# Self-attention's last two units: low parts, two 16-bit copies a unit and the weight splits laid out again on VectorE

## What is computed

```python
q = proj(w_q); k = proj(w_k); v = proj(w_v)
qn = _rmsnorm(q, q_gamma) * dh ** (-0.5)
kn = _rmsnorm(k, k_gamma)
sim = jnp.einsum('bhid,bhjd->bhij', qn, kn)
attn = jax.nn.softmax(sim, axis=-1)
out = jnp.einsum('bhij,bhjd->bhid', attn, v)
```

## Time before and its profile

| | us |
|---|---|
| median of 3 runs | 2266.23 (2263.83 to 2267.96) |
| the profiled execution | 2270.32 |
| its span | 2268.5 |
| PE busy | 2161.2 |
| ACT busy | 1606.2 |
| DVE busy | 1567.6 |
| POOL busy | 1451.5 |
| L599, low parts on POOL, x448 | 952.9 |
| L934, low parts on DVE, x32 in batch 0 | 40.4

### The profile page before, as it was taken

The page is one execution under the profiler, slowest core; times in us unless marked ns, Lnnn a source line. Parts: engine busy times, 40 slices in busy tenths (PEclk is TensorE's granted clock), DMA queues, the critical chain, the costliest instruction groups (busy, mean ns, idle before and its releaser), DMA issues. The chain is left out here.

```text
span 2268.5 us, 62703 instructions
## 1 busy us (share of the span) xinstructions
PE 2161.2 (95%) x22392; PEld 1243.8 (55%) x22392; DVE 1567.6 (69%) x2601; ACT 1606.2 (71%) x1831; POOL 1451.5 (64%) x1010
## 2 busy tenths in 40 slices
PE   6999999999997999999999999999999978998999
PEld 3545666666664455444445456666666644554444
DVE  6997777777776666753379977777777766677522
ACT  4557999999997566631146489999999965666210
POOL 3425889888887586721234178889888975866210
PEclk9999999999999999999999999999999999999999
DMA  5210000000002202102122100000000031020000
GB/s 108 65 42 1 11 0 9 9 9 9 9 9 63 64 2 48 38 21 73 43 63 64 28 2 10 9 0 9 9 9 9 10 89 38 2 62 24 20 24 33
DMA packets 102349, 65.24 MB, mean 29 GB/s; under 512 B 75346, under 2 KB 75346, under 8 KB 102226
## 3 DMA queue, kind: packets, MB, share of 16 engines
q1 hardware_dynamic: 102226, 63.57, 12.7%
HBM read 46.69 MB, written 8.39 MB: 24 GB/s over the span
## 5 line engine op out<-in xcount | busy, mean ns | idle before, releaser
L599 POOL TENSOR_TENSOR qkn<-wide 128x1024 f16<-128x1024 f32 x448 | 952.9, 2155 | 140.2 <-PE bank L716 124.1
L920 DVE TENSOR_REDUCE sq<-bank 128x1 f32<-128x512 f32 x1024 | 685.3, 688 | 216.3 <-PE bank L668 209.7
L845 ACT ACTIVATE wide<-bank,shift 128x1024 f32<-128x1024 f32 x512 | 571.4, 1116 | 14.5 <-POOL qkn L599 6.5
L837 ACT ACTIVATE wide<-bank,shift 128x1024 f16<-128x1024 f32 x512 | 569.1, 1112 | 9.1 <-PE bank L684 9.1
L683 PE MATMUL bank<-q_hh,ko 128*128 (+1 forms) x1024 | 388.7, 380 | 13.1 <-ACT wide L845 13.0
L668 PE MATMUL bank<-ko,q_hh 128*128 (+1 forms) x1024 | 386.8, 380 | 9.2 <-DVE sq L920 5.9
L684 PE MATMUL bank<-q_lm,k_h 65*128 (+1 forms) x1024 | 389.0, 380 | 0.0
L701 PEld LDWEIGHTS bank<-v_hl,wide 128*128 128x128 f16 x4096 | 287.6, 98 | 63.3 <-issue 5.6
L701 PE MATMUL bank<-v_hl,wide 128*128 (+1 forms) x4096 | 319.8, 192 | 0.1
L703 PE MATMUL bank<-v_hl,wide 128*128 (+1 forms) x4096 | 318.2, 193 | 0.0
L703 PEld LDWEIGHTS bank<-v_hl,wide 128*128 128x128 f16 x4096 | 267.5, 96 | 58.7
(11 more groups left out here) (227 smaller groups left out, 4177.4 us busy)
## 6 DMA issues: line engine op xcount, KB each, us to landing
wide<-in_x SPq DMA_DIRECT2D x32, 256.0 KB, 2.7
q_lm<-in_x SPq DMA_DIRECT2D x32, 256.0 KB, 3.2
ko<-in_L_ffn_W SPq DMA_DIRECT2D x32, 256.0 KB, 4.0
q_hh<-q_hh SPq DMA_DIRECT2D x32, 128.0 KB, 2.6
ko<-k_h SPq DMA_DIRECT2D x32, 128.0 KB, 2.8
out<-bo_b SPq DMA_DIRECT2D x16, 256.0 KB, 2.0
out<-xbo_b SPq DMA_DIRECT2D x16, 256.0 KB, 2.0
q_lm<-sq SPq DMA_DIRECT2D x248, 0.2 KB, 4.9
```

The costliest lines, as they stand in the source:

```text
L599: pool.tensor_tensor(probs_l[:, p % 2, :], probs[:, p % 2, :], probs_h[:, p % 4, :], ALU.subtract).then_inc(pl_pool, 1)
L837: act.activation(probs_h[:, p % 4, :], SB[p % 2][:, :], ACT.Exp, bias=shift[:, 0:1]).then_inc(ph_ready, 1)
L845: act.activation(probs[:, p % 2, :], SB[p % 2][:, :], ACT.Exp, bias=shift[:, 0:1]).then_inc(p_ready, 1)
L920: dve.tensor_reduce(pm[:, s, k:k + 1], MB[k % 2], AX_X, ALU.max).then_inc(mx_free, 1)
```

## The change

In units 30 and 31 of each batch, and nowhere else:

- DVE makes all 8 low parts (`end_unit`); POOL's loop ends after unit 29.
- ACT leaves out the float16 exponential of pairs 2 and 5 (`COPIES`); DVE makes that high part by a `tensor_copy` from the float32 exponential.
- The four steps of two weight splits (high, low, high, low) no longer stand behind the unit but behind the low parts of pairs 1, 2, 4 and 5.
- The division of the unit before stands behind the low part of pair 1.
- ACT's loop ends after unit 29 and the last two units are written out. New semaphores `ph_end` and `pl_end` count the copies and low parts there.

```diff
-                        with pool.Fori(0, UNITS) as u:
+                        with pool.Fori(0, MAXED) as u:
...
                         def values_high(u, p, ob):
-                            pe.wait_ge(ph_ready, (U0 + u) * PAIRS + p + 1)
+                            if at_end(u) and p in COPIES:
+                                pe.wait_ge(ph_end, end_copy(u, p))
+                            else:
+                                pe.wait_ge(ph_ready, high_count(u, p))
...
                         def values_low(u, p, ob):
 
-                            if p == DVE_PAIR:
-                                pe.wait_ge(pl_dve, U0 + u + 1)
+                            if at_end(u):
+                                pe.wait_ge(pl_end, end_low(u, p))
+                            elif p == DVE_PAIR:
+                                pe.wait_ge(pl_dve, b * MAXED + u + 1)
...
-                        with act.Fori(0, UNITS) as u:
+                        def exps(u):
                             G = (U0 + u) * PAIRS
                             for p in range(PAIRS):
                                 act.wait_ge(s_ready, G + p + 1)
-                                act.activation(probs_h[:, p % 4, :], SB[p % 2][:, :], ACT.Exp, bias=shift[:, 0:1]).then_inc(ph_ready, 1)
-
-                                if p - 2 == DVE_PAIR:
-                                    act.wait_ge(pl_dve, U0 + u + 1)
+                                if not (at_end(u) and p in COPIES):
+                                    act.activation(probs_h[:, p % 4, :], SB[p % 2][:, :], ACT.Exp, bias=shift[:, 0:1])\
+                                        .then_inc(ph_ready, 1)
+
+                                if at_end(u) and p >= 2:
+                                    act.wait_ge(pl_end, end_low(u, p - 2))
+                                elif at_end(u) and u > MAXED:
+                                    act.wait_ge(pl_end, end_low(u - 1, PAIRS - 2 + p))
+                                elif p - 2 == DVE_PAIR:
+                                    act.wait_ge(pl_dve, b * MAXED + u + 1)
...
+                        with act.Fori(0, MAXED) as u:
+                            exps(u)
+                        for u in range(MAXED, UNITS):
+                            exps(u)
...
+                        def end_unit(u, s, pieces):
+
+                            for p in range(PAIRS):
+                                G = (U0 + u) * PAIRS + p
+                                dve.wait_ge(p_ready, G + 1)
+                                if p in COPIES:
+                                    dve.tensor_copy(probs_h[:, p % 4, :], probs[:, p % 2, :]).then_inc(ph_end, 1)
+                                    dve.wait_ge(ph_end, end_copy(u, p))
+
+                                dve.wait_ge(lo_done, G + 1)
+                                dve.tensor_tensor(probs_l[:, p % 2, :], probs[:, p % 2, :], probs_h[:, p % 4, :], ALU.subtract)\
+                                    .then_inc(pl_end, 1)
+                                if p == 1:
+                                    output(u - 1, 1 - s)
+                                if p in (1, 2, 4, 5):
+                                    split_part(pieces[p // 4], p in (2, 5))
...
-                        unit(MAXED, 0, maxed=False)
-                        split_both(PIECES_P3[0:2])
-                        unit(MAXED + 1, 1, maxed=False)
-                        split_both(PIECES_P3[2:4])
+                        end_unit(MAXED, 0, PIECES_P3[0:2])
+                        end_unit(MAXED + 1, 1, PIECES_P3[2:4])
                         output(UNITS - 1, 1)
```

More of the change, by code:

```diff
@@ L227, in decoder_layer @@
         ph_ready = sem("ph_ready")
+        ph_end = sem("ph_end")
+        pl_end = sem("pl_end")
         p_ready = sem("p_ready")
@@ L499, in decoder_layer, with at_end, end_low, end_copy @@
                     next_l = {"o": share4[2], "xq": share4[3]}
+                    COPIES = (2, 5)
+                    HIGHS = MAXED * PAIRS + (UNITS - MAXED) * (PAIRS - len(COPIES))
                     def low_count(u, p):
-                        return (U0 + u) * (PAIRS - 1) + (p if p < DVE_PAIR else p - 1) + PAIRS
+                        return b * (MAXED * (PAIRS - 1)) + u * (PAIRS - 1) + (p if p < DVE_PAIR else p - 1) + PAIRS
+                    def at_end(u):
+                        return isinstance(u, int) and u >= MAXED
+                    def end_low(u, p):
+                        return (b * (UNITS - MAXED) + u - MAXED) * PAIRS + p + 1
+                    def end_copy(u, p):
+                        return (b * (UNITS - MAXED) + u - MAXED) * len(COPIES) + COPIES.index(p) + 1
+                    def high_count(u, p):
+                        if at_end(u):
+                            return b * HIGHS + MAXED * PAIRS + (u - MAXED) * (PAIRS - len(COPIES)) + p + 1 \
+                                - sum(q < p for q in COPIES)
+                        return b * HIGHS + u * PAIRS + p + 1
                     def turned(t):
@@ L949, in output, with split_part @@
                                 .then_inc(o_free, 1)
[L951 to L955, removed]
+                        def split_part(piece, low):
+                            w = PIECES.index(piece)
+                            slot, nth, _ = use[w]
+                            if low:
+                                split_low(dve, b, [piece], stage3, next_h, next_l)
+                            else:
                                 dve.wait_ge(w_loaded[slot], b * (32 * taken[slot]) + 32 * nth)
@@ L958, in split_both, with unit @@
                                                   WS, None, ALU.mult).then_inc(wh_ready, 1)
-                                split_low(dve, b, [piece], stage3, next_h, next_l)
-                        def unit(u, s, first=False, maxed=True):
+                        def end_unit(u, s, pieces):
[12 more added lines that the diff above has]
+                                    split_part(pieces[p // 4], p in (2, 5))
+                        def unit(u, s, first=False):
                             if first:
@@ L966, in unit @@
                             for k in range(16):
-                                if maxed:
-                                    reduce_max(u + LA, k, s)
+                                reduce_max(u + LA, k, s)
                                 if k == 4 and not first:
@@ L972, in unit @@
                                     probs_low(u)
-                            if maxed:
-                                negate_max(u + LA, s)
+                            negate_max(u + LA, s)
                         dve.tensor_copy(eye16[:, :], ident[:, :]).then_inc(e_eye, 1)
```

## The result

| | before | changed |
|---|---|---|
| median, us | 2266.23 (5 runs, 2263.83 to 2267.96) | 2253.14 (5 runs, 2248.27 to 2254.54) |
| profiled execution, us | 2270.32 | 2248.27 |
| its span, us | 2268.5 | 2246.5 |

By the medians the change brings 13.1 us, where 15.4 were forecast (2251). The ratio over all runs is 0.9937, with a 95% interval of 0.9926 to 0.9948, that is 14.3 us, between 11.8 and 16.8.

A forecast was written before the change was run, and what follows sets the result against it. Taken to bound the last two units: ScalarE's and GpSimd's queues, then a GpSimd and SyncE tail. Gain 2 x 7.7 = 15.4 us: profiled 2270.32 to 2254.9, less 4.09 for the median, 2250.8, forecast 2251; range 2245 to 2260.

The forecast's parts named there:

- What bounded the stretch: Units 30 and 31: ScalarE's and GpSimd's queues, then a GpSimd and SyncE tail; 8.6 us from last exponential's start to next stage.
- Prices: VectorE's work in units 30 and 31: low part 1.13 us, copy 0.71 (upper end 1.2), 14.51 us a unit.
- rival A: VectorE in units 30 and 31 costs more than its bare rows: gain 8.5 to 12.5 us, 2253.7 to 2257.7; chance 0.25.
- Rival C: VectorE's low parts in units 30 and 31 stay at 1.91 us, slowed by ScalarE's writes: 2271.8 us; chance 0.05.
- The hand-over: Units 30 and 31: ScalarE waits 1.28 us before pair 5, VectorE 0.31 + 0.87 at unit 31's start; period 15.69 us.
- The boundary: End of self-attention: SyncE's issues end before the division, PE starts 0.45 us behind it, 7.7 us earlier a batch.
- Rival D: Next stage waits for its own transfers at a fixed time, so the early end is lost: 2266 us; chance 0.06.
- The sum: Both batches' last two units together: 2 x 7.7 = 15.4 us gained, giving 2251 us.

The follow-up runs named there:

- e5: Kernel before, with only the weight splits spread around pair 4's low part and GpSimd still making its low parts: 2267.28 us, ratio 1.0002.
- e8: The changed kernel itself, run and profiled again without edits: 2254.54 us, ratio 0.9947 to the kernel before.
- e1: Changed kernel without the two copies, ScalarE making all 16 exponentials of units 30 and 31: 2252.38 us, ratio 0.9933.
- e3: Changed kernel without copies and with the splits behind the unit again, leaving only all low parts on VectorE: 2264.86 us, ratio 0.9983.
- e4: Changed kernel plus 11 idle-time matmuls of 512 columns on PE at the end of self-attention: 2252.83 us, ratio 0.9933.
- e7: Changed kernel with one copy a unit instead of two, plus 11 idle-time matmuls at the end of self-attention: 2246.88 us, ratio 0.9910.

## Why the prediction was right

**What bounded the stretch.** The claim was two queues, ScalarE's and GpSimd's, with a tail of GpSimd and SyncE. The profile after bears it out: with GpSimd gone, ScalarE runs at 1.00 us an exponential, and the tail from the last exponential's start to the next stage is 4.4 us instead of 8.6.

**Prices.** The copy, for which no row stood, took 0.683 to 0.685 us in all 8 cases, and its follower started 0.71 or 0.72 us after it: the value taken, not the 1.2 of the upper bound. The Trainium skill ("VectorE: DVE Perf Modes", section "What auto-detection actually checks") puts an instruction with a single source and destination in SBUF into the faster mode, whether it is a copy or the high step; the trace agrees, 0.684 against 0.68. The low part came 1.14 us apart instead of 1.13. So rival A, every instruction a little dearer, has nothing to show for it in these units.

**Rival C** (low parts as dear as 1.91) is ruled out by 1.222 as the median of 32. With e5 it can be said why they had been dear: VectorE's low step takes 3.03 us beside GpSimd whether it stands early or late in the unit, and 1.22 without it, while ScalarE writes on in both. The prediction leaves one thing out: only the first high step of each unit was free at 0.68, as GpSimd did not run again until 699.90 and 718.50, and of each pair of splits before the change the second high step took 2.6 us. With GpSimd idle all of them take 0.68 (691.28 to 712.93 above). The source view of the kernel before:

```profile
L957 DVE TENSOR_SCALAR share<-q_lm x8: 679/1644/2616, 699.7 to 1844.8; 128x1024 f16<-128x1024 f32 x8
```

The rule of the Trainium skill ("SBUF — State Buffer", section "Who interferes with whom") names the same pair of engines.

**The hand-over.** Gaps of 1.28 and 0.31 + 0.87 us were forecast, 1.22 and 0.26 + 0.78 measured. Period 15.69, measured 15.80.

**The boundary.** SyncE's issues off the path, the division last, PE 0.45 us behind: 0.34 measured. Sum 7.7 a batch, 7.6 measured. Rival D is out: the landmarks of the next stage move with its start (first row maxima of batch 0 30.8 us behind it, 30.7 before).

**The sum.** 15.4 was forecast; the last two units gave 15.2 in the profile, self-attention as a whole 14.7 and, in e8, 14.3. The difference lies in units 0 to 29, which the change does not touch: from the start of self-attention to unit 30 batch 1 took 526.3 us (526.4 in e8) against 525.7 before, batch 0 525.3 (525.4) against 525.4. The medians gave 13.1 and 12.3 in two series, the ratios 14.3 and 12.0, with intervals that reach to 16.8 and 15.0. What is missing, 1 to 3 us, is by subtraction outside self-attention, where the clock falls in other places from execution to execution. No run settles whether it is chance, and the intervals do not exclude that nothing is missing.

**What the prediction did not say.** It let the two copies stand as a price worth paying, without asking what the change would be without them. Its own balance, 14.51 us for VectorE against 14.0 for ScalarE, held the answer: with none it is 13.1 against 16.0, and the period about the same (15.80 measured with the copies, 16.02 in e1). The gain is low parts away from GpSimd and splits spread, and neither does it alone. So the forecast sum is right for the kernel as laid out, but one of its three parts, the copies, contributes next to nothing to it.

## What to carry to other kernels

When two engines hand tiles to each other through two buffers, ask how far their queues are from level before moving work from one to the other: here four exponentials a batch moved away brought 0.1 us, and the place of the copies between two hand-overs 1.4. Test the parts of a change alone and in pairs: here one part brought 3 us (e3), one nothing (e5), and the two together 15.6 (e1). And look at what stands behind the last instruction that matters: four DMA issues that waited for a weight split ended a stage 1.3 us after all arithmetic was done.

## What the runs showed of the hardware

- Beside GpSimd's float32 subtractions, VectorE's two-input instruction on 128x1024 in SBUF takes 1.99 to 3.03 us instead of 1.22, the one-input high step up to 2.62 instead of 0.68, and GpSimd's own 2.30 to 2.68 on the mean of a run instead of 2.09: both lose. Spreading VectorE's steps over more of GpSimd's run only spread the loss (e5).
- The granted clock can be held over a stage boundary by 11 matmuls of 512 columns, 11 x 0.22 = 2.4 us of PE's time in its own waiting time. The granted clock is 1.00 in every window over the boundary in e4 and e7, and falls there in all other runs. The Trainium skill says in general that throttled is the default and that activity releases it ("TensorE: Matmul & The Clock Gate", section "What's actually happening"); e4 and e7 agree. Of what it gives at the stage's start, 1.6 and 2.0 us a batch by its first row maxima, e4's whole time shows little: ScalarE then waited 2.82 us for a weight for which it had not waited, and the clock fell elsewhere (34 us of the stages at half clock, against 36 in e8).
- Execution to execution, the stages behind self-attention differed by up to 9 us (964.8 to 973.7) in ten profiles of nearly the same code, and the time at half clock (23 to 55 us) goes with it. A single profiled pair can thus show 22 us where the medians show 13.
